# A post-norm attention and NF4 feed-forward layer on one core: feed-forward in four groups, other seams between the stages, and eight unread products per attention group

## The reference

```python
B, S, E = 4, 512, 512;  H, D = 32, 16;  HID = 1376
q, k, v = x @ wq.T + bq, x @ wk.T + bk, x @ wv.T + bv        # (B, S, H, D)
scores = einsum('bshd,bstd->bsht', q, k) / sqrt(D)           # between the heads of one token
context = einsum('bsht,bstd->bshd', softmax(scores), v)
x = layernorm(x + context)
w1, w2, w3 = nf4_quant_dequant(w1), ...                      # per block of 64: nearest of 16 levels x absmax
x = layernorm(x + (silu(x @ w1.T) * (x @ w2.T)) @ w3.T)
```

## Time and profile before

| | us |
|---|---|
| median of 3 runs | 825.99 (825.88 to 828.45) |
| the profiled execution's own time | 828.94 |
| its span | 827.1 |
| TensorE busy | 738.1 |
| VectorE busy | 631.5 |
| ScalarE busy | 469.5 |
| GpSimd busy | 112.5 |

### The profile page before, as it was taken

The page is one execution under the profiler, slowest core; times in us unless marked ns, Lnnn a source line. Parts: engine busy times, 40 slices in busy tenths (PEclk is TensorE's granted clock), DMA queues, the critical chain, the costliest instruction groups (busy, mean ns, idle before and its releaser), DMA issues.

```text
span 827.1 us, 14113 instructions
## 1 busy us (share of the span) xinstructions
PE 738.1 (89%) x5668; PEld 629.3 (76%) x5668; DVE 631.5 (76%) x844; ACT 469.5 (57%) x599; POOL 112.5 (14%) x91
## 2 busy tenths in 40 slices
PE   2898989893989989999699799979899999999993
PEld 1776868673989988999588587858787888877782
DVE  1597989785988898887669999999999983314544
ACT  1477878674663745636287677757687672112221
POOL 2002021425000000100002120120111000001111
PEclk9999999995555655655589899989999999999997
DMA  9942635499989596993535223513241431224304
GB/s 190 248 123 96 189 129 160 138 233 243 252 186 247 139 273 151 246 250 114 189 106 202 81 75 106 178 54 129 69 147 46 140 130 46 102 103 119 85 13 89
DMA packets 88752, 120.27 MB, mean 145 GB/s; under 512 B 24656, under 2 KB 69968, under 8 KB 85616
## 3 DMA queue, kind: packets, MB, share of 16 engines
q1 hardware_dynamic: 86960, 116.23, 49.7%
q10 hardware_dynamic: 1728, 3.15, 1.7%
HBM read 80.55 MB, written 38.80 MB: 144 GB/s over the span
## 4 chain that ended last, share of the span: by engine, by line
PE 57%; DVE 23%; issue 9%; ACT 5%; DMA 3%; SPq 1%; ACTq 1%; DVEq 0%
DVE nf_acc L1028 14%; PE ps_p L905 12%; PE ps_p L822 7%; PE ps_p L824 7%; PE ps_p L823 7%; PE ps_s L822 6%; PE ps_s L823 6%; PE ps_s L824 6%; PE ps_s L892 4%; ACT nf_y L666 3%; PE ps_t L843 2%; DMA wst<-in_L_attn_wq 1%; DVE part L1166 1%; SPq L481 1%; DVE f_lb L1046 1%
## 5 line engine op out<-in xcount | busy, mean ns | idle before, releaser
L1028 DVE SCALAR_TENSOR_TENSOR nf_acc<-nf_y,nf_acc 128x1024 f32<-128x1024 f32 (+3 forms) x238 | 298.6, 1255 | 44.0 <-ACT nf_y L666 36.1
L666 ACT ACTIVATE nf_y<-nf_w,bound_b 128x1024 f32<-128x1024 f32 (+3 forms) x255 | 280.8, 1130 | 18.7 <-DVE nf_acc L1028 18.0
L905 PE MATMUL ps_p<-probT,v_bd 128*68 128x32 f32 x1024 | 125.5, 300 | 2.6 <-DVE probT L1077 2.5
L905 PEld LDWEIGHTS ps_p<-probT,v_bd 128*68 128x68 f32 x1024 | 122.6, 211 | 4.1 <-issue 2.6
L822 PE MATMUL ps_s<-x_hl,f_ha 128*128 128x512 f32 (+1 forms) x224 | 88.5, 395 | 0.0
L822 PE MATMUL ps_p<-x_hl,w_hl 128*128 128x512 f32 x192 | 79.2, 412 | 10.0 <-DVE x_hl L1046 8.7
L823 PE MATMUL ps_s<-x_hl,f_ha 128*128 128x512 f32 (+1 forms) x224 | 87.9, 392 | 0.0
L824 PE MATMUL ps_s<-x_hl,f_la 128*128 128x512 f32 (+1 forms) x224 | 87.6, 391 | 0.0
L1191 DVE TENSOR_TENSOR silu<-silu,ps_s 128x512 f32<-128x512 f32 (+1 forms) x44 | 29.9, 680 | 74.8 <-PE ps_s L824 74.7
L809 ACT ACTIVATE hid_hl<-silu 128x512 fp32r<-128x512 f32 (+1 forms) x44 | 27.8, 632 | 86.1 <-DVE silu L1191 85.3
L824 PE MATMUL ps_p<-x_hl,w_hl 128*128 128x512 f32 x192 | 76.5, 399 | 0.0
(11 more groups left out here) (92 smaller groups left out, 1255.3 us busy)
## 6 DMA issues: line engine op xcount, KB each, us to landing
x_hl<-x_parts SPq DMA_DIRECT2D x12, 2048.0 KB, 8.7
qk_parts<-qk_p SPq DMA_DIRECT2D x64, 204.0 KB, 2.5
q_st<-qk_parts SPq DMA_DIRECT2D x48, 272.0 KB, 6.6
k_st<-qk_parts SPq DMA_DIRECT2D x48, 272.0 KB, 7.5
x_parts<-x_st SPq DMA_DIRECT2D x16, 512.0 KB, 4.1
nf_w<-in_L_ffn_w SPq DMA_DIRECT2D x24, 256.0 KB, 3.1
dequantised<-nf_acc SPq DMA_DIRECT2D x10, 512.0 KB, 4.1
part<-in_L_attn_hidden_states SPq DMA_DIRECT2D x8, 512.0 KB, 12.7
```

Of the source, the lines that this page charges most:

```text
L666: act.activation(nf_y[0:p, at % NY, 0:w], nf_w[0:p, u % 2, 0:w], ACT.Identity, bias=bound_b[0:p, i:i + 1], scale=STEEP).then_inc(s_ny, 1)
L905: t = pe.matmul(ps_p[0:MV, (G + 3) % NPV, i * H:(i + 1) * H], v_bd[hb % 2][:, :, g * GI + i], probT[:, G % 2, i], start=True, stop=True)
L1028: dve.scalar_tensor_tensor(out=acc, in0=y, scalar=float(NF4[i + 1]), in1=acc, op0=ALU.min, op1=ALU.max).then_inc(s_nacc, 1)
```

## The change

It has several parts.

- Start: the loads of wq, wk and the first input block are issued half by SP and half by ScalarE, in that order; the first feed-forward weights come behind the biases. `load_x` and `load_w` become helpers of both engines.
- Projection: turns may use four banks (`ps_t` and `ps_s`) and stand one projection earlier for the next block (`P_TURNS`). `NV` is 4. `LV_P` sums to 64 levels and not 59.
- Attention: `fill` puts `FILL` = 8 bf16 products of 32 x 512 before the values of each group but the last two. They write partitions 96 to 127 of the bank that the values then use; nothing reads them.
- Seam behind attention: two units instead of four are turned before the first step; the last block's "ct" and "xt" turns, moments and norm and two units move into steps 0 to 6.
- Feed-forward: four groups of 4, 4, 2 and 1 slices, with the blocks in alternating direction, so that 10 loads of x1 remain of 12; there are 16 block sums instead of 12 and 19 units instead of 17 (the four for w3 in the last groups are 576 and 256 columns wide). `LV_F` holds 3 or 4 levels in steps 0 to 6, 5 in 7 to 14, 4 in 15 to 31, and 6 narrow ones in 32 to 37.
- End: the shift for the second norm is computed quarter by quarter.

```diff
-    GROUPS = [range(0, 4), range(4, 8), range(8, NJ)]
+    GROUPS = [range(0, 4), range(4, 8), range(8, 10), range(10, NJ)]
...
+    ORDER = [(g, b if g % 2 == 0 else NBK - 1 - b) for g in range(len(GROUPS)) for b in range(NBK)]
...
+    for n in range(1, NBL):
+        DRAIN_AT.setdefault(FIRST_STEP[n] + 1, []).append(n - 1)
+    DRAIN_AT.setdefault(NS, []).append(NBL - 1)
...
-    NQK, NV, NPV = 5, 3, 4
+    NQK, NV, NPV = 5, 4, 4
+    FILL = 8
...
-    LV_P = [1, 1, 1, 1, 1, 1, 1, 1, 1, 2, 2, 2] * NBK
-    LV_P[:4] = [0, 1, 1, 1]
+    LV_P = [1, 1, 1, 1, 1, 1, 1, 1, 2, 2, 2, 2] * NBK
...
-    LV_F = [(2, 3)] * (8 * NJG) + [(0, 0)] * (NS - 8 * NJG)
+    LV_F = [(1, 2)] * 4 + [(2, 2)] + [(1, 2)] * 2 + [(2, 3)] * 8 + [(2, 2)] * (FIRST_OF[2] - 15) + [(3, 3)] * 6
+    LV_F += [(0, 0)] * (NS - len(LV_F))
...
+                P_TURNS.setdefault(3 * KC * b + 2 * KC - 1 + c, []).append(("x", b + 1, c))
...
-    TAIL_2 = [("f", u, s) for u in W_UNITS[:1] for s in range(2)]
-    TAIL_3 = [("f", u, s) for u in W_UNITS[1:] for s in range(2)]
-    TURNS += TAIL_1 + TAIL_2 + [("ct", NBK - 1, k) for k in range(len(HEADS))] + TAIL_3
-    F_TURNS = {0: [("xt", NBK - 1, 0), ("xt", NBK - 1, 1)], 1: [("xt", NBK - 1, 2), ("xt", NBK - 1, 3)]}
+    TAIL_2 = [("f", u, s) for u in W_UNITS[:2] for s in range(2)]
+    TURNS += TAIL_1 + TAIL_2
...
+    F_TURNS = {0: [("f", W_UNITS[2], 0), ("f", W_UNITS[2], 1), CT_LAST[0]],
+               1: [("f", W_UNITS[3], 0), ("f", W_UNITS[3], 1), CT_LAST[1]],
+               2: CT_LAST[2:4], 3: CT_LAST[4:], 5: XT_LAST[:2], 6: XT_LAST[2:]}
+    MOMENTS_F, NORM_F = 3, 4
...
         def turn_bank(key):
-            return ps_t[:, TURN[key] % 2]
+            n = TURN[key]
+            if n < NPT:
+                return (ps_t, ps_s)[n % 4 // 2][:, n % 2]
+            return ps_t[:, n % 2]
...
-            load_x(0)
-            load_unit()
+            for q in range(2):
+                load_w(sp, 0, q)
+            load_x(sp, 0, 0)
+            for q in range(2):
+                load_w(sp, 1, q)
...
-            load_w(0)
-            load_w(1)
+            for q in range(2, Q4):
+                load_w(act, 0, q)
+            load_x(act, 0, 1)
+            for q in range(2, Q4):
+                load_w(act, 1, q)
...
+            def fill(G):
+
+                hb = G // NG
+                if G % NG == 0:
+                    pe.wait_ge(s_ldv[hb % 2], 16 * Q4 * (hb // 2 + 1))
+                wait(pe, s_ctx, G - NPV + 1)
+                some = v_bd[hb % 2][:].bitcast(BF16)
+                for _ in range(FILL):
+                    pe.matmul(ps_p[96:128, (G + 3) % NPV].rearrange("p (a t) -> p a t", t=TI), some[:, 0, 1:TI:2],
+                              some[:, 0:8, 1:2 * TI:2], start=True, stop=True)
...
                 if G >= 2:
+                    fill(G - 2)
                     values(G - 2)
...
-                if n >= 2 * NBK:
-                    for q in range(Q4):
-                        a = Q4 * b + q + 1
-                        dve.wait_ge(s_rstd2, a)
+                        if q:
+                            shift_2(a - 1, q - 1)
```

More of the change, by code:

```diff
@@ L82, in layer_kernel, with turns_of @@
     NU0 = len(GROUPS[0]) + 2
+    def turns_of(u):
+        kind, g, _ = UNITS[u]
+        return [("f", u, s) for s in range(2 if kind == "w" else -(-len(GROUPS[g]) // 2))]
     def valid(g):
@@ L345, in down_over @@
         def down_over(eng, step):
-            n = BLOCK_OF[step]
+            n = STEPS[step][0]
             if step == LAST_STEP[n]:
@@ L440, in reload @@
                 sp.wait_ge(s_dst, 16 * (u + 1))
+                if g == 1 and kind == "t":
+                    x1_stored(sp, NBK - 1)
+                if g >= 2:
+                    sp.wait_ge(s_sum, Q4 * NBK * (g - 1))
                 if kind == "w":
@@ L469, in _ @@
             load_unit()
-            for b in range(1, NBK):
-                load_x(b)
+            sp.wait_ge(s_tr, TURN[("w", 0, KC - 1)] + 1)
+            for q in range(2):
+                load_w(sp, 2, q)
+            for e in range(2):
+                load_x(sp, 1, e)
+            load_unit()
+            for b in range(2, NBK):
+                for e in range(2):
+                    load_x(sp, b, e)
             sp.wait_ge(s_pad, 1)
@@ L760, in _ @@
                 i, m = divmod(k, KC)
-                if b == 0 and i < 2:
-                    high(("w", i + 1, m))
-                elif b + 1 < NBK and i == 2:
-                    high(("x", b + 1, m))
+                for key in P_TURNS.get(tau, []):
+                    high(key)
                 if i < 2:
@@ L810, in _ @@
                 for key in F_TURNS.get(s, []):
-                    high(key)
+                    if key[0] != "ct":
+                        high(key)
+                if s == NORM_F:
+                    norm_1(NBK - 1)
                 steep(LV_F[s][1])
-                if g == 2 and b and s == FIRST_STEP[BLOCK_OF[s]] + 1:
-                    for q in range(Q4):
-                        norm_2(b - 1, q)
-            for q in range(Q4):
-                norm_2(NBK - 1, q)
+                for m in DRAIN_AT.get(s, []):
+                    if m >= LAST_G:
+                        for q in range(Q4):
+                            norm_2(m, q)
+            for m in DRAIN_AT[NS]:
+                for q in range(Q4):
+                    norm_2(m, q)
         @block.tensor
@@ L1120, in _ @@
                 i, m = divmod(k, KC)
-                if b == 0 and i < 2:
-                    low(("w", i + 1, m))
-                elif b + 1 < NBK and i == 2:
-                    low(("x", b + 1, m))
+                for key in P_TURNS.get(tau, []):
+                    low(key)
                 if i < 2:
@@ L1151, in _ @@
                 low(key)
-            for k in range(len(HEADS)):
-                add_context(("ct", NBK - 1, k))
-            moments(NBK - 1)
-            for key in TAIL_3[:2]:
-                low(key)
-            mean_shift(NBK - 1)
-            for key in TAIL_3[2:]:
-                low(key)
             def drain(n):
-                b = n % NBK
+                b = ORDER[n][1]
                 for q in range(Q4):
@@ L1196, in _ @@
                 for key in F_TURNS.get(s, []):
-                    low(key)
+                    if key[0] == "ct":
+                        add_context(key)
+                    else:
+                        low(key)
+                if s == MOMENTS_F:
+                    moments(NBK - 1)
                 lift(LV_F[s][1])
-            drain(3 * NBK - 1)
+            for m in DRAIN_AT[NS]:
+                drain(m)
 _INS = ["L0_attn_hidden_states", "L0_attn_wq", "L0_attn_bq", "L0_attn_wk", "L0_attn_bk", "L0_attn_wv",
```

185 lines of the change are left out of this document (101 added, 84 removed).

## The result

The changed kernel takes 865.15 us (median, 861.15 to 866.72) where the kernel before takes 825.93 us in the same session: ratio 1.0462, 95% interval 1.0418 to 1.0505. It is slower by 4.6%; the two medians are 39 us apart. Forecast were 880 us and a range of 830 to 897. The profiled execution took 863.94 us.

The account below looks back on a forecast made before the run. Attention was taken as bound by TensorE, the first feed-forward piece largely paced by VectorE. The terms 91 - 9 - 4 - 8 - 14.6 - 4 + 2 = +53.4 on the 825.99 us median gave 879.4, stated as 880 us, range 830 to 897.

Parts of the forecast that it names:

- likeliest case: Clock mostly low in attention, with the case that it never rises included: 862 to 897 us, chance 0.67.
- Part A: Attention: eight added products per group lie on TensorE's path, mostly at low clock: 96 us, less 5 absorbed, +91.
- full-clock rival: Attention: the extra products keep the clock up throughout and the transposes halve: 829 us, chance 0.15 (820 to 838).
- "half-high" rival: Attention: the clock is high in half of the groups: near 855 us, chance 0.11 (840 to 862).
- "Never rises": Attention: products with 32 output columns are too little to raise the clock: 102 us, time 887, within the 0.67 case.
- "hidden": Attention: extra products run beside values or the scores' tail: near 783 us if hidden wholly, chance 0.07 (under 820).
- B: Start: wq and the first input block arrive sooner, first projection near 17.6 us: -9 us (bounds 0 and -12).
- C: Projection: earlier transposes, four banks deep, win back 4 of 17 us of waiting: -4 us (bounds -10 and +4).
- D: First seam: a fourth v_t buffer ends ScalarE's 9.73 us wait: -8 us (bounds 0 and -9.7).
- E: Second seam: only two more units stand before the first gate product: -14.6 us (bounds -8 and -15).
- F: Feed-forward: 387 us after, 391.3 before, with moved turns and fewer levels in many steps: -4 us (bounds -14 and +8).
- G: End: blocks 14 and 15 drained in a row on VectorE, less normalising by quarters: +2 us (bounds -2 and +6).

Follow-up runs that it names:

- a1_no_fill: The changed kernel without the eight unread products per attention group: 803.19 us, ratio 0.9702 to the kernel before.
- a4_interleaved: The changed kernel with the same eight products per group, one before every second value product instead of all before the values: 946.41 us, ratio 1.1424.
- n3_two_inputs: a1_no_fill with the first level of each unit as a VectorE instruction with two inputs: 801.77 us, ratio 0.9688.
- n1_levels: a1_no_fill with eight levels moved out of the last two projections and first two attention groups into later attention groups: 808.06 us, ratio 0.9763.
- n4_nv3: a1_no_fill with three buffers of v_t instead of four: 802.30 us, ratio 0.9703.
- n6_units_back: a1_no_fill with the two feed-forward weight units of steps 0 and 1 turned before the first step again: 799.00 us, ratio 0.9652.
- n2_three: a1_no_fill with three feed-forward groups of 4, 4 and 3 slices instead of four: 801.10 us, ratio 0.9672.

## Why the prediction was right, and where it was not

The sign and the range held, and the time lies in the interval of the likeliest case (862 to 897), 15 us below the forecast. That is partly luck: two errors of opposite sign cancel in part. Part A was too dear by 30.8 us by the spans, and the rest too good by 12.4 (parts B to G: -37.6 forecast; a1_no_fill shows -25.2, with 2.6 of that in attention itself). Of the signs named, the clock (0.80, not 0.5 to 0.7) and the length of the attention stage (257 us, not 285) came out otherwise, and the sign of being wrong, products 0.22 us apart, was there for about half of them.

- **A, mis-sized.** Forecast were 96 us for the products, less 5 absorbed; measured are 60.2. The step that failed is "most extra products start at the low level", 3.2 us a group. In the trace a set is busy 2.77 us, half way between the 3.60 of a low and the 1.97 of a high one, and takes 2.66 without the overlap of record ends: 80 us and not 96. The clock did fall between sets, as forecast from the earlier trace rows, before 21 of 30; but in 18 of these it rose inside the set, and for stretches of several groups it did not fall at all. A term was put at nothing: the transposes in attention, 6.5 us cheaper, which the forecast counted only in the full-clock rival. The rest of the 30.8 is 3.3 for the first set in a wait that was there anyway, 1.4 more idle time filled (6.4, forecast 5), and the 3.3 outside attention that a1_no_fill doesn't explain. So the truth lies nearest to the "half-high" rival (chance 0.11), not to the forecast; its 855 would have been near had the seams given what was expected.
- **The rivals.** "Never rises" fell (clock 0.80), "hidden" fell (a4_interleaved), "full clock" came nearest to true with 128 columns: 849, and not 829, since the seams gave 12 us less and the clock was 0.88; and that run isn't the change. By the rule of the Trainium skill, "TensorE: Matmul & The Clock Gate", section "Why this matters for your kernels", that the forecast set against its own, the time would be 838. The trace doesn't bear it out: TensorE is busy 256.2 of 256.8 us in attention, at 0.80.
- **Value and score products gain nothing from the clock**: right. 3.9 us and 1.3 us a group at either level.
- **B**, -9: right (-9.7). **C**, -4: -7.2, within its bounds.
- **D**, -8 (bounds 0 and -9.7): wrong, +0.6. The wait for v_t was the last to end before, and is gone; but behind it stood VectorE's level beside GpSimd (n3_two_inputs) and behind both the second stacks (n1_levels). I named two levels as next late and left them no more than the 1.7 us between 9.7 and 8. n4_nv3 shows that the fourth buffer gives nothing with these two in place.
- **E**, -14.6: -15.3, right in size (0.3 beyond the bound), but n6_units_back shows that the part of it that comes from the two units was a bad trade: 5 us won in the seam, up to 10 lost in the steps.
- **F**, -4: -0.5. What it lacked is the waits of steps 0 and 1 just named; waits for drains in this part shrank as expected (5.52, now at most 2.82) and waits for reloaded weights came (3.08, 2.28).
- **G**, +2: +6.3, just outside the bounds. The two drains in a row were seen, but not that the first starts only behind the last step's hidden values. From 842.29 on the two take 15.5 us of VectorE in a row; it waits only for a result of GpSimd, 0.66 us, behind each, so the saving that the forecast took for what would run beside TensorE didn't come. TensorE's low clock in the stretch (0.63) holds up none of this: VectorE never waits for it there. n2_three, with one drain behind the last product, has 16.0 us.

## What to carry to other kernels

A wait taken away is worth the distance to the next one; look for that one by its own row, an instruction's place beside another engine's included, and not by the instruction's usual length. Work put in to lift the clock has to be paid from instructions that the clock makes faster: here those were 25 us of transposes, of which the clock gave back 6.5, against 83 us of added products. Turns moved from a seam into steps paced by VectorE are not free: try both places.

## What the runs showed of the hardware that was not expected

- TensorE was occupied 96% of the attention stretch without the unread products and still ran at a mean clock of 0.54. Eight products of 512 columns among 5.1 us of small ones brought 0.80 with 32 or 0.82 with 64 output columns, and 0.88 with 128; the same eight one at a time between values brought 0.55.
- A level of VectorE with one input was held 9.77 us by three GpSimd instructions in a row; with two inputs it took 2.99 us, and the next three 1.4 us each, beside the memsets.
- An unread product between two pairs of value products cost 0.67 us, in a block of eight at the low clock 0.43.
